# Attention after group norm on one core: the column maximum of a half's scores in one VectorE pass in place of seven

## The reference

```python
xn = group_norm(x, gamma, beta)              # 32 groups, statistics over all tokens of an image
q, k, v = xf @ wq + bq, xf @ wk + bk, xf @ wv + bv
scores = jnp.einsum('bnc,bmc->bnm', q, k) * C ** (-0.5)
attn = jax.nn.softmax(scores, axis=-1)
out = jnp.einsum('bnm,bmc->bnc', attn, v) @ wp + bp
return out.reshape(B, H, W, C) + residual
```

## Time and profile before

| | us |
|---|---|
| median of 3 runs | 2093.55 (2093.4 to 2094.18) |
| the profiled execution | 2094.07 |
| its span in the trace | 2092.3 |
| TensorE busy | 2085.0 |
| VectorE busy | 1730.5 |
| ScalarE busy | 743.5 |
| GpSimd busy | 538.4 |

### The profile page before, as it was taken

The page is one execution under the profiler, slowest core; times in us unless marked ns, Lnnn a source line. Parts: engine busy times, 40 slices in busy tenths (PEclk is TensorE's granted clock), DMA queues, the critical chain, the costliest instruction groups (busy, mean ns, idle before and its releaser), DMA issues.

```text
span 2092.3 us, 28020 instructions
## 1 busy us (share of the span) xinstructions
PE 2085.0 (100%) x9215; PEld 1725.9 (82%) x9215; DVE 1730.5 (83%) x2834; ACT 743.5 (36%) x1221; POOL 538.4 (26%) x236
## 2 busy tenths in 40 slices
PE   9999999999999999999999999999999999999999
PEld 7888888888888888888888888888888888888887
DVE  7997888878888788897878888788887888878864
ACT  4342433325233252332423333243332523325231
POOL 1322223221232212322223231222322123221231
PEclk9999999999999999999999999999999999999999
DMA  6212020120301203021030211202112030120201
GB/s 177 61 43 78 1 87 33 50 70 10 93 18 50 70 10 110 0 73 47 25 95 0 80 40 43 77 0 88 33 50 70 10 94 17 50 70 12 69 1 61
DMA packets 110332, 108.13 MB, mean 52 GB/s; under 512 B 8541, under 2 KB 74081, under 8 KB 110305
## 3 DMA queue, kind: packets, MB, share of 16 engines
q1 hardware_dynamic: 108544, 104.63, 16.4%
q10 hardware_dynamic: 1760, 3.15, 0.6%
HBM read 74.19 MB, written 33.55 MB: 51 GB/s over the span
## 4 chain that ended last, share of the span: by engine, by line
PE 99%; DVE 1%; ACT 0%; DMA 0%; issue 0%; POOL 0%; SPq 0%; DVEq 0%
PE psum L1328 11%; PE psum L1309 11%; PE psum L1310 11%; PE psum L1311 11%; PE psum L1330 11%; PE psum L1329 11%; PE psum L1124 6%; PE psum L1122 6%; PE psum L1123 6%; PE psum L1218 5%; PE psum L1216 5%; PE psum L1219 5%; PE psum L1290 0%; PE psum L1291 0%; PE psum L1292 0%; PE psum L1144 0%
## 5 line engine op out<-in xcount | busy, mean ns | idle before, releaser
L447 POOL TENSOR_TENSOR x_res<-x_res,out_bias 128x512 f32<-128x512 f32 x124 | 215.3, 1760 | 899.4 <-PE psum L1219 453.0
L1328 PE MATMUL psum<-v_hi,pt_hi 128*128 128x512 f32 x1024 | 398.5, 389 | 0.0
L1329 PE MATMUL psum<-v_lo,pt_hi 128*128 128x512 f32 x1024 | 398.4, 389 | 0.0
L1330 PE MATMUL psum<-v_hi,pt_lo 128*128 128x512 f32 x1024 | 398.4, 389 | 0.0
L583 ACT ACTIVATE score<-psum 128x512 f32<-128x512 f32 x256 | 152.6, 596 | 325.4 <-PE psum L1311 325.4
L1330 PEld LDWEIGHTS psum<-v_hi,pt_lo 128*128 128x128 f32 x1024 | 192.2, 188 | 40.0
L1329 PEld LDWEIGHTS psum<-v_lo,pt_hi 128*128 128x128 f32 x1024 | 192.2, 188 | 39.8
L1328 PEld LDWEIGHTS psum<-v_hi,pt_hi 128*128 128x128 f32 x1024 | 192.2, 188 | 39.8
L1309 PE MATMUL psum<-pt_hi,xn_hi 128*128 128x512 f32 x512 | 199.3, 389 | 0.0
L1123 PE MATMUL psum<-m_lo,xn_hi 128*128 128x512 f32 x512 | 199.2, 389 | 0.0
L1124 PE MATMUL psum<-m_hi,xn_lo 128*128 128x512 f32 x512 | 199.2, 389 | 0.0
(11 more groups left out here) (163 smaller groups left out, 3945.2 us busy)
## 6 DMA issues: line engine op xcount, KB each, us to landing
x_res<-in_x_dram SPq DMA_DIRECT2D x128, 256.0 KB, 2.8
out_dram<-x_res SPq DMA_DIRECT2D x128, 256.0 KB, 2.1
x_blk<-in_x_dram SPq DMA_DIRECT2D x240, 128.0 KB, 2.9
score<-in_x_dram SPq DMA_DIRECT2D x16, 128.0 KB, 7.2
w_q<-in_L_conv_wq_dram ACTq DMA_DIRECT2D x6, 256.0 KB, 8.7
w_v<-in_L_conv_wv_dram SPq DMA_DIRECT2D x1, 1024.0 KB, 9.5
w_p<-in_L_conv_wp_dram SPq DMA_DIRECT2D x1, 1024.0 KB, 8.2
w_k<-in_L_conv_wk_dram ACTq DMA_DIRECT2D x4, 256.0 KB, 6.8
```

What stands on the lines that cost most here:

```text
L447: last = nc.gpsimd.tensor_tensor(at, at, out_bias[:, first:end], ALU.add)
L1328: nc.tensor.matmul(dst, hi[:, m, queries], v_hi[:, m, :], start=m == 0, stop=False)
L1329: nc.tensor.matmul(dst, hi[:, m, queries], v_lo[:, m, :], start=False, stop=False)
L1330: end = nc.tensor.matmul(dst, lo[:, m, queries], v_hi[:, m, :], start=False, stop=m == NT - 1)
```

## The change

The seven two-input maximum steps of a half, each on one more tile as soon as it was copied out, become one `tensor_reduce` over the half's eight tiles. It reads `score[h]` with the tile index innermost (512 elements, 2 KB, from each word to the next), 4096 words in each partition, and writes 512. It stands behind the wait for the half's last copy. `s_mx` now counts one step for a half in place of seven, and GpSimd waits for that.

```diff
             def await_top_part(n, h):
-                pool.wait_ge(s_mx, (n * NH + h + 1) * (NT - 1))
+                pool.wait_ge(s_mx, n * NH + h + 1)
...
-            def top_part_step(n, h, m):
-                dve.wait_ge(s_sr, (n * NH + h) * NT + m + 1)
-                if m == 1:
-                    if not starts(n, h):
-
-                        dve.wait_ge(s_par, n * NH + h)
-                elif m > 1:
-                    dve.wait_ge(s_mx, (n * NH + h) * (NT - 1) + m - 1)
-                if m:
-                    nc.vector.tensor_tensor(top_part[h][:], score[h][:, 0, :] if m == 1 else top_part[h][:],
-                                            score[h][:, m, :], ALU.max).then_inc(s_mx, 1)
+            def top_parts(n, h):
+
+                dve.wait_ge(s_sr, (n * NH + h + 1) * NT)
+                if not starts(n, h):
+
+                    dve.wait_ge(s_par, n * NH + h)
+                nc.vector.tensor_reduce(top_part[h][:], score[h][:].rearrange("p m n -> p n m"),
+                                        mybir.AxisListType.X, ALU.max).then_inc(s_mx, 1)
...
                 for m in range(NT):
-                    if more and m == NT - 1:
-                        dve.wait_ge(s_sv, (b + 1) * STAT_STEPS + 1)
-                    top_part_step(b, 0, m)
                     if more:
+
+                        dve.wait_ge(s_sr, b * NH * NT + m + 1)
                         for q in TRANSPOSED.get(m, ()):
                             quarter_transpose(b + 1, q)
                         if m in MEASURED:
                             token_stats(b + 1, *MEASURED[m])
                     if starts(b) and m in (4, 5):
                         first_residual(m - 4)
+                if more:
+                    dve.wait_ge(s_sv, (b + 1) * STAT_STEPS + 1)
+                top_parts(b, 0)
                 if more:
                     channel_stats(b + 1)
...
                 for m in range(NT):
-                    top_part_step(b, 1, m)
                     if 1 <= m <= KC:
                         total_part_steps(b, 0, 2 * m - 2, 2 * m)
                     if 3 <= m < 3 + KC:
                         pt_lo_parts(b, 0, 2 * m - 6, 2 * m - 4)
+                top_parts(b, 1)
                 for m in range(2, NT - 1):
```

## The result

| | before | after |
|---|---|---|
| median | 2093.86 us (2093.4 to 2094.19, 4 runs) | 2150.31 us (2147.2 to 2150.61, 4 runs) |
| ratio | | 1.0266 (95% interval 1.0254 to 1.0278) |
| profiled execution, its span | 2094.07, 2092.3 | 2150.07, 2148.3 |

The account below looks back on a forecast made before the run. TensorE, busy 2085.0 of 2092.3 us, was taken to bound the kernel. Waits of 1.07 and 0.55 us an image made 26 us over 16 images, 27 with first and last adjusted: 2121 us, range 2092 to 2160.

Parts of the forecast that it names:

- What bounds the kernel, and that the change can only cost: TensorE, busy 2085.0 of 2092.3 us, never waits in the 16 images, so the change can gain nothing there, only add waits.
- T: Duration of the new VectorE reduction pass over 4096 words a partition, one for each half; taken as 7.0 us.
- the middle between two bounds: Price per word of the pass, 1.65 ns, midway between 1.04 (neighbouring words) and 2.25 (slowest steady rate); gives 6.9 us.
- The first place: Half 0: TensorE's ("s", 1, 5) needs the bank that ScalarE's late copy of ("s", 1, 1) empties; wait 1.07 us an image.
- the delay D: Half 0: how much later what stands behind the pass on VectorE starts, T - 1.87, so 5.1 us at T = 7.0.
- The second place: Half 1: TensorE's ("v", 0, 6) needs VectorE's `v_lo` of ("v", 0, 2), queued behind the pass; another 0.5 us an image.
- "0.05 to 0.1 us to wake up": In half 0, TensorE's wake-up after ScalarE's copy, 0.05 to 0.1 us, leaving 4.1 us of cover.
- "The granted clock should stay at its full level": TensorE's clock was to stay full since pauses are of a microsecond; if it fell, the cost would exceed the waits.
- The first image, "about 2 us more": Two more 512-element additions between pass and shift, 1.2 us; TensorE waits about 2 us more in its two places.
- The last image, "about 1 less": The last image has no statistics to stand behind, so TensorE was to wait about 1 us less.
- The half-rate rival: Each word of the pass costs two cycles, 2.08 ns: T = 8.7, 5.0 us an image, 2175 us; chance 0.22.
- The GpSimd rival: GpSimd's sum in half 1 might start later than counted and hold back that half's shift; chance 0.02.

## Why the prediction was right and wrong

- *What bounds the kernel, and that the change can only cost:* right. The version with full-rate reads stands within 0.1% of the kernel before, for the reason given, that TensorE waits nowhere.
- *T, by the middle between two bounds, 7.0 us:* the bounds 4.4 and 9.4 held it, and the lower one is exact (4.42). **This is the step that failed first.** The middle was a choice between two bounds and not a price, and the measured 7.51 is 0.5 above it. By the prediction's own slope, 2 us an image for each microsecond, that is 1.0 us an image, 16 us: with T at 7.51 its sum gives 43 us in place of 27, and that is the largest share of the miss. A lone pass takes 7.03, which the middle met by luck, and TensorE beside it adds 0.47. Neither could be had from rows of a kernel without a strided read. The estimate of 7.2 from the Trainium skill's figure was nearer to the pass in its place.
- *The first place:* right in mechanism. By T - 1.87 the delay D would be 5.64 at the measured T; ScalarE's wait grew from 4.20 to 10.11, by 5.91. By the prediction's working TensorE would wait 1.58 us; it lost 1.79, since the pass also starts 0.16 us later behind its last copy than was counted.
- *The second place:* right in mechanism, and the halves run apart show the chain that the prediction drew, the second place opened by the delay of the first. By its working 1.06 us at T = 7.51; the bracket has 0.79, and with the 0.16 that it leaves out 0.95.
- *"0.05 to 0.1 us to wake up", and nothing else for a pause:* **the second step that failed.** The wake-up is right: the copy ends at 1155.15 and TensorE starts at 1155.20. What the sum put at nothing is the other half of the restart, the slower starts behind a pause, some 0.16 us each and 5 us for the 31 pauses. With the clock, next, that makes 10 us.
- *"The granted clock should stay at its full level":* wrong, three times, with 1.5 to 1.7 us each by the 0.83 to 0.85 of 10 us windows, some 5 us. The prediction said that the cost would then exceed the waits, and so it is.
- *The first image, "about 2 us more":* its brackets are 2.50 and 1.10 us, 1.2 more than in a middle image. *The last image, "about 1 less":* its brackets are 0.66 and 3.01, 1.2 more; wrong at the second place. There GpSimd's sum runs beside VectorE's low parts, as it did before, and six of them take 5.74 us, in a middle image 3.69; the pass starts 2.0 us later for it, and TensorE waits 3.01 us.

The sum: 40.7 us in the two wait rows, 10 of restart and 5 of clock are the 56; the last two are also what TensorE's busy time rose by, 14.8. In the prediction's own terms: 27, 16 for T, 3 for waits a little longer than its working gives, 5 for slower starts and 5 for the clock. The half-rate rival (2175, T = 8.7) is out by the row of the pass; at its T = 9.4 the working gives 6.4 us an image and 2196, not 6.3 and 2194. The range's upper end, 2160, held, but with some luck: 2150 is the forecast's own time for a T of about 7.9, so the room left for a dearer pass took up the cost of the pauses.

One reading was off without a consequence: 683 ns is the mean step of half 1. The six later steps of half 0 take 1027 in the mean (98.6 us for 96); no term of the sum uses them.

The GpSimd rival had no part: its maximum of half 1 started 0.3 us behind the pass and was done 6 us before the shift that needs it.

## What to carry to other kernels

What a late pass costs is its length behind the last input, against the cover of the engine that bounds the kernel: here 4.4 us were covered and 7.5 were not, and the same 7.5 us were covered in half 1 alone. Follow such a delay along every engine's queue to each place where the bounding engine stands behind it, and count them as gates of one delay: opening the first alone moved the wait to the second and made the kernel slower still. On VectorE, choose an order of words with steps of 4 or 8 bytes for a float32 reduction, or price the pass at 1.7 to 1.8 ns a word, and at 2.4 where the step is 24 words. Count a pause of the bounding engine at more than its length: here each cost 0.3 us more, and 1.7 more where the clock fell.

## What was not expected of the hardware

- A VectorE reduction of float32 reads at 1.04 ns a word for steps of 1 and 2 words, 1.77 to 1.79 at 4 and 8, 1.67 at 16, 2.43 at 24 and 1.68 from 32 to 512.
- A strided pass is slowed by its neighbours where one over neighbouring words is not: 7.03 us alone, 7.50 with TensorE's matmuls beside it, 7.19 with ScalarE's copies. The other takes 4.41 alone and 4.42 with matmuls beside it.
- Pauses of TensorE of 5.2 us brought its clock to 1.2 GHz in every image, for 3.4 and 6.8 us in the windows shown, and the fall came before the pause was over. Pauses of 2.63 us did so in some images and not in others, one of 1.92 us in one kernel and not in another; pauses of 1.63 and 0.80 us never in the changed kernel.
